# A two-part graph network kernel: PSUM columns in node order, one contiguous one-hot per edge tile

## The reference

```python
def _layer(h, src, dst, norm, n_nodes, W, b, g, be):
    h = h @ W
    msg = h[src] * norm[:, None]
    h = jax.ops.segment_sum(msg, dst, num_segments=n_nodes) + b
    h = jnp.tanh(h)                      # then LayerNorm, * g + be
...
h = jnp.maximum(_layernorm(x), 0.0)
x = x + gcn(h)                           # two _layer, with self loops
h = jnp.maximum(_layernorm(x), 0.0)
msg = jax.nn.relu(h[src] + edge_attr)
aggr = jax.ops.segment_sum(msg, dst)
out = x + (h + relu(relu((h + aggr) @ W1 + b1) @ W2 + b2))
```

## Time and profile before

| | |
|---|---|
| median of 3 runs | 2902.43 us (2901.16 to 2912.98) |
| profiled execution | 2900.96 us, span 2899.1 us |
| busy | PE 2130.6, DVE 2363.1, ACT 2021.1, POOL 1765.8 us |
| granted clock of PE, mean over the span | 0.892 |
| edge multiplications (L1237) | 7500, in two groups of 3750: 1044.3 and 1013.4 us busy |
| one-hots (L918) | 1875, 860.8 us busy |
| DMA | 446.67 MB in 234,030 packets |

### The profile page before, as it was taken

The page is one execution under the profiler, slowest core; times in us unless marked ns, Lnnn a source line. Parts: engine busy times, 40 slices in busy tenths (PEclk is TensorE's granted clock), DMA queues, the critical chain, the costliest instruction groups (busy, mean ns, idle before and its releaser), DMA issues.

```text
span 2899.1 us, 53761 instructions
## 1 busy us (share of the span) xinstructions
PE 2130.6 (73%) x15433; PEld 1913.3 (66%) x15433; DVE 2363.1 (82%) x8137; ACT 2021.1 (70%) x5708; POOL 1765.8 (61%) x2717
## 2 busy tenths in 40 slices
PE   0200039999999957677767778787179999999988
PEld 0100039998889957676667677786168888887877
DVE  4999847887777747999999999999968787777665
ACT  0039967998899666555666666546488999988756
POOL 4025667777777537887667756762077776765540
PEclk9999999999999779777888877768689999999869
DMA  0059945665556443444445444433256665655443
GB/s 14 1 218 381 371 156 144 178 176 169 162 173 178 114 163 108 128 129 142 149 146 146 138 136 152 142 109 124 106 149 176 183 178 173 168 167 156 141 115 102
DMA packets 234030, 446.67 MB, mean 154 GB/s; under 512 B 98093, under 2 KB 99128, under 8 KB 233732
## 3 DMA queue, kind: packets, MB, share of 16 engines
q1 hardware_dynamic: 189193, 374.34, 38.6%
q0 software_dynamic: 43680, 68.58, 11.2%
q10 hardware_dynamic: 859, 0.23, 0.0%
HBM read 286.58 MB, written 156.41 MB: 153 GB/s over the span
## 4 chain that ended last, share of the span: by engine, by line
PE 43%; DVE 35%; ACT 11%; POOL 5%; issue 3%; DMA 2%; SPq 1%; DVEq 0%; ACTq 0%
PE ps L1237 21%; DVE hot_ L918 9%; ACT rows_f_ L1053 6%; PE ps L1272 6%; PE ps L1282 6%; PE ps L1222 5%; PE ps L1253 5%; POOL got_f_ L682 5%; DVE stat_b_ L853 4%; DVE stat_a_ L853 4%; DVE rows_f_ L980 4%; DVE y_f_ L972 2%; DVE hot_p_ L747 2%; DVE low_f_ L892 2%; DVE square_f L833 1%
## 5 line engine op out<-in xcount | busy, mean ns | idle before, releaser
L682 POOL DMA_INDIRECT got_f_<-table,src_of x1365 | 1424.7, 1044 | 751.0 <-issue 370.5
L1237 PE MATMUL ps<-hot_,high_f_ 128*96 128x304 f32 (+46 forms) x3750 | 1044.3, 313 | 285.9 <-DVE hot_ L918 283.9
L1237 PE MATMUL ps<-hot_,low_f_ 128*96 128x304 f32 (+46 forms) x3750 | 1013.4, 308 | 0.0
L1237 PEld LDWEIGHTS ps<-hot_,high_f_ 128*96 128x96 f32 (+1 forms) x3750 | 704.1, 188 | 360.0 <-issue 195.4
L918 DVE TENSOR_SCALAR hot_<-node_at,dst_of 128x368 fp32r<-128x368 f32 (+33 forms) x1875 | 860.8, 498 | 46.7 <-PE ps L1237 42.3
L1237 PEld LDWEIGHTS ps<-hot_,low_f_ 128*96 128x96 f32 (+1 forms) x3750 | 706.5, 188 | 32.0
L1066 ACT COPY z_f_<-ps 97x1024 f32<-97x1024 f32 (+2 forms) x294 | 301.1, 1024 | 365.5 <-PE ps L1237 364.6
L1078 ACT ACTIVATE y_f_<-ps,ds 128x96 f32<-128x96 f32 x1568 | 388.6, 377 | 104.5 <-PE ps L1253 104.4
L1222 PE MATMUL ps<-ident_f,in_f_ 128*97 128x128 f32 (+1 forms) x1568 | 226.3, 292 | 265.3 <-DMA in_f_<-table 265.3
L853 DVE BATCH_NORM_STATS2 stat_a_<-y_f_ 128x6 f32<-128x96 f32 x1952 | 385.7, 245 | 5.9 <-ACT y_f_ L1078 5.8
L1222 PEld LDWEIGHTS ps<-ident_f,in_f_ 128*97 128x97 f32 (+1 forms) x1568 | 198.5, 181 | 265.6 <-DMA in_f_<-table 265.6
(11 more groups left out here) (117 smaller groups left out, 2807.7 us busy)
## 6 DMA issues: line engine op xcount, KB each, us to landing
x_f_<-in_x SPq DMA_DIRECT2D x146, 384.0 KB, 3.9
table<-rows_f_ SPq DMA_DIRECT2D x98, 396.0 KB
in_f_<-table SPq DMA_DIRECT2D x98, 396.0 KB
table<-rows_f_ SPq DMA_DIRECT2D x98, 392.0 KB
in_f_<-table SPq DMA_DIRECT2D x98, 392.0 KB
table<-rows_f_ SPq DMA_DIRECT2D x98, 388.0 KB
in_f_<-table SPq DMA_DIRECT2D x98, 388.0 KB
out<-y_f_ SPq DMA_DIRECT2D x97, 384.0 KB, 4.5
```

The source lines that it names most:

```text
L682: pool.indirect_dma_start(out=got_f[g][:, u * w:(u + 1) * w], out_offset=None, in_=table[:, :], in_offset=bass.IndirectOffsetOnAxis(ap=src ...
L1237: last = pe.matmul(acc[0:w, h, :].rearrange("m (s p) -> m s p", p=P)[:, :, p0:p0 + pw], part[:, u * wide_w:u * wide_w + w], hot_view(slot, ...
```

## The change

PSUM's columns are put in the order of the nodes. For that a partition now holds 4 nodes of the first half of the block (4p to 4p + 3) and 4 of the second (512 + 4p on): the loads and stores move two runs of 4 rows for each partition (`move`), and the degrees' positions are computed with other shifts. A slab is then every fourth column of a bank: the own transposes write PSUM with a stride of 4 words (16 bytes), and the projection and output layer read their weights with that stride. A tile has one contiguous one-hot over its band (cut at block borders only where the band is wider than 1024 nodes), which serves all blocks that the tile touches; its buffer is free again after the last of them. PE multiplies one contiguous piece for each bank that the tile touches, twice for high and low. Bands are rounded to 2 nodes.

```diff
-                lo = max(first, int(lo) // (2 * slabs) * 2 * slabs)
-                hi = min(stop, -(-math.ceil(hi) // (2 * slabs)) * 2 * slabs)
+                lo = max(first, int(lo) // 2 * 2)
+                hi = min(stop, -(-math.ceil(hi) // 2) * 2)
...
-                    for b in range(lo // block, -(-hi // block)):
-                        p0, p1 = (max(lo, b * block) - b * block) // slabs, (min(hi, (b + 1) * block) - b * block) // slabs
-                        use.append((place[b], q, u, b, p0, p1 - p0))
+                    cuts = [lo, hi] if hi - lo <= block else [lo, *range((lo // block + 1) * block, hi, block), hi]
+                    for lo, hi in zip(cuts, cuts[1:]):
+                        k = len(self.tiles)
+                        self.tiles.append((q, u, lo, hi))
+                        use += self.uses(place, block, k, lo, hi)
...
+    def uses(self, place, block, k, lo, hi):
+        found = []
+        for b in range(lo // block, -(-hi // block)):
+            pieces = []
+            for h in range(2):
+                bank = b * block + h * block // 2
+                c0, c1 = max(lo, bank), min(hi, bank + block // 2)
+                if c0 < c1:
+                    pieces.append((h, c0 - bank, c1 - c0, c0 - lo))
+            found.append((place[b], k, pieces))
+        return found
...
+        def move(eng, i, table, tile, done, load, whole=True):
+            lo = plan.at[i] * BLOCK
+            if whole or lo + BLOCK <= N:
+                far = table[ds(lo, BLOCK), :].rearrange("(h p q) d -> p h (q d)", h=2, q=S // 2)
+                near = tile[:, :, :].rearrange("p (h q) d -> p h (q d)", h=2)
+                eng.dma_start(near if load else far, far if load else near).then_inc(done, 16)
+                return
+            ...
+        def slab_cols(t, h):
+            return t[:, h * HB:(h + 1) * HB].rearrange("m (p q) -> m q p", q=S // 2)
...
-                for m in plan.pairs_at[i]:
-                    q, u, b, p0, pw = plan.pairs[m]
-                    slot, turn = hot_slot(layer, m)
+                for k in plan.tiles_at[i]:
+                    q, u, lo, hi = plan.tiles[k]
+                    slot, turn = hot_slot(layer, k)
...
                     if turn >= HOTS:
-                        dve.wait_ge(pair_done, turn - HOTS + 1)
+                        b_layer, b_k = divmod(turn - HOTS, TILES)
+                        dve.wait_ge(pair_done, b_layer * PAIRS + plan.last_of[b_k] + 1)
                     c = plan.quads[q][1] + u
-                    dve.tensor_scalar(hot_view(slot, pw), node_at[:, :, 0:pw], float(b * BLOCK + p0 * S),
-                                      dst_of[:, c:c + 1], ALU.add, ALU.is_equal).then_inc(hot_ready_f, 1)
+                    dve.tensor_scalar(hot[slot][:, 0:hi - lo], node_at[:, 0:hi - lo], float(lo), dst_of[:, c:c + 1],
+                                      ALU.add, ALU.is_equal).then_inc(hot_ready_f, 1)
...
-                    k = s % 4 * P
-                    last = pe.matmul(acc[0:w, s // 4, k:k + P], own[:, s, 0:w], ident_f[:, :], start=s % 4 == 0,
+                    to = acc[0:w, s // 4, :].rearrange("m (p q) -> m q p", q=S // 2)[:, s % 4, :]
+                    last = pe.matmul(to, own[:, s, 0:w], ident_f[:, :], start=s % 4 == 0,
...
-                    for h in range(2):
+                    for h, c0, n, a in pieces:
                         for part in (high_f[f], low_f[f]):
-                            last = pe.matmul(acc[0:w, h, :].rearrange("m (s p) -> m s p", p=P)[:, :, p0:p0 + pw],
-                                             part[:, u * wide_w:u * wide_w + w],
-                                             hot_view(slot, pw)[:, h * S // 2:(h + 1) * S // 2, :],
+                            last = pe.matmul(acc[0:w, h, c0:c0 + n], part[:, u * wide_w:u * wide_w + w],
+                                             hot[slot][:, a:a + n], start=False,
...
-                    last = pe.matmul(to[:, s // 4, s % 4 * D:(s % 4 + 1) * D], z_f[i % 2][0:w, s * P:(s + 1) * P],
+                    last = pe.matmul(to[:, s // 4, s % 4 * D:(s % 4 + 1) * D], slab_cols(z_f[i % 2][0:w, :], s // 4)[:, s % 4, :],
...
-                    last = pe.matmul(ps[3][:, s // 4, s % 4 * D:(s % 4 + 1) * D], hid_f[i % 2][:, s * P:(s + 1) * P],
+                    last = pe.matmul(ps[3][:, s // 4, s % 4 * D:(s % 4 + 1) * D], slab_cols(hid_f[i % 2], s // 4)[:, s % 4, :],
```

More of the change, by code:

```diff
@@ L130, in __init__ @@
         self.first_place = [place[b] for b, _ in supers]
-        self.quads, self.pairs, self.pairs_at, use = [], [], [[] for _ in range(blocks)], []
+        self.quads, self.tiles, self.pairs, self.pairs_at, use = [], [], [], [[] for _ in range(blocks)], []
         for i in self.order:
@@ L209, in gnn_kernel @@
     TILES_MAX = CHUNK
+    TILES = len(plan.tiles)
+    assert all(plan.last_of[k - HOTS] < plan.first_of[k] for k in range(HOTS, TILES))
+    assert max(hi - lo for _, _, lo, hi in plan.tiles) <= BLOCK
     assert GROUPS4 == 4 and SUPERS <= 128 and all(plan.pairs_at) and plan.at.index(BLOCKS - 1) >= X_RING + Y_RING
@@ L507, in table_written, with moved, hot_slot @@
                 eng.wait_ge(stored[j], stored_before(stage + 1, j))
[L509 to L514, removed]
+        def move(eng, i, table, tile, done, load, whole=True):
[5 more added lines that the diff above has]
+                return
+            for h in range(2):
+                rows_n = min(HB, N - lo - h * HB)
+                parts = rows_n // (S // 2)
+                far = table[ds(lo + h * HB, rows_n), :].rearrange("(p q) d -> p (q d)", q=S // 2)
+                near = tile[0:parts, h * (S // 2):(h + 1) * (S // 2), :].rearrange("p q d -> p (q d)")
+                eng.dma_start(near if load else far, far if load else near).then_inc(done, 16)
+        def moved(i, ring):
+            turns = range(i % ring, i + 1, ring)
+            return 16 * (len(turns) + (plan.at.index(BLOCKS - 1) in turns))
+        def hot_slot(layer, k):
+            n = layer * TILES + k
             return n % HOTS, n
+        def slab_cols(t, h):
+            return t[:, h * HB:(h + 1) * HB].rearrange("m (p q) -> m q p", q=S // 2)
         def quad_slot(layer, q):
@@ L625, in fast_sync @@
                     sp.wait_ge(out_done, k + 1)
-                    parts = parts_at(k)
-                    sp.dma_start(rows(out, plan.at[k], parts),
-                                 y_f[k % Y_RING][0:parts, :, :].rearrange("p s d -> p (s d)")
-                                 ).then_inc(out_stored[k % Y_RING], 16)
+                    move(sp, k, out, y_f[k % Y_RING], out_stored[k % Y_RING], False, whole=False)
             for j in range(Y_RING):
-                sp.wait_ge(out_stored[j], 16 * len(range(j, BLOCKS, Y_RING)))
+                sp.wait_ge(out_stored[j], moved(BLOCKS - 1 - (BLOCKS - 1 - j) % Y_RING, Y_RING))
         def prologue_pool(pool):
@@ L1229, in gather_edges @@
                 for m in plan.pairs_at[i]:
-                    q, u, _, p0, pw = plan.pairs[m]
-                    slot, turn = hot_slot(layer, m)
+                    k, pieces = plan.pairs[m]
+                    q, u, _, _ = plan.tiles[k]
+                    slot, turn = hot_slot(layer, k)
                     f, quad_turn = high_slot(layer, q)
```

50 lines of the change are left out of this document (24 added, 26 removed).

## The result

The changed kernel takes 3457.6 us (median of 4 runs, 3448.9 to 3461.0) against 2901.9 for the kernel before on the same chip: ratio 1.191, 95% interval 1.188 to 1.193. The forecast was 2852 with a range from 2822 to 3005. The rival nearest to the time, strided weights at half rate, had a chance of 0.18 and said 3207 (about 3350 if strided transposes cost as much too); the time lies above both. The counts came out as worked out (5382 edge multiplications, 1644 one-hots). The profiled execution has a span of 3454.9.

The account below looks back on a forecast made before the run. No engine bounds the whole: ACT and DMA fill stage 0, POOL paces layer 0, DVE layer 1, PE layer 2. Terms -10 - 17 - 26 + 3 = -50 gave 2901 - 50 + 1.5: 2852 us, range 2822 to 3005.

Parts of the forecast that it names:

- strided weights at half rate: Rival: projection and output-layer weight loads double; +136, +30, +136 us in layers 0, 1, 2, giving 3207 us; chance 0.18.
- Strides, PE: PE's strided transpose writes to PSUM and strided weight loads in projection and output layer: no cost, 0 taken.
- The end that I gave, doubling: Upper end for PE's strides: 85 us a layer for transposes, 168 us a layer for weights.
- A new wait: DVE waits for one-hot buffers held until a tile's last block; layer 1, bounds 0 and 15 us, 3 taken.
- the 3 us: Cost taken in layer 1 for one-hot buffers held into a second block.
- what the sum said: All terms together, over stage 0 and three layers: -50 us.
- I take 10, bounds 3 and 20: Layer 0, paced by POOL: 10 us saved in the tail and a quicker follow-up to late gathers.
- Layer 1: 17: 17 us saved: 10 from fewer DVE one-hots, 7 from the block of 43 tiles; bounds 5 to 25.
- Layer 2: 26: 26 us saved from fewer PE edge multiplications, with ACT close behind; bounds 15 to 38.
- Stage 0: +3: Loading node rows in smaller DMA pieces costs 3 us, bounds 0 and 15.

Follow-up runs that it names:

- experiment 1: The changed kernel with contiguous weight loads again, the 16-byte stride moved to ACT's copy out of PSUM: 3026.4 us, ratio 1.043.
- experiment 4: The kernel before with projection and output-layer weights read at every second word (8 bytes): 2913.7 us; at every eighth word (32 bytes): 3432.0 us.
- experiment 3: The kernel before with only the own transposes writing PSUM at every fourth word: 2899.6 us, ratio 0.999.
- the two numbered kernels: Tiles numbered in building order, in the change with strided weights (3262.9 us) and in the change with contiguous weights and ACT's strided copy (2846.3 us).
- Experiment 2: The kernel before with only projection and output-layer weights read at every fourth word (16 bytes): 3382.0 us, ratio 1.165.
- renumbered change: The changed kernel, strided weights kept, with its tiles numbered in the order DVE builds them: 3262.9 us, ratio 1.124.
- experiments 6 and 7: Tiles numbered in building order: contiguous weights 2846.3 us, the change 3262.9, cut at blocks 2854.4; old numbers, contiguous weights, only PE's wait count mended: 2857.5 us.

## Why the prediction was wrong

Three parts make the result, each from two kernels: strided weights 3262.9 - 2846.3 = +417; numbering 3457.6 - 3262.9 = +195; and the rest of the change 2846.3 - 2900.2 = -54. Together +558, against 3457.6 - 2901.9 = +556. The parts hardly depend on their order: with the old numbering the strides cost 431 (experiment 1), and without them the numbering costs 180.

**The step that failed: "*Strides, PE* ... I take 0", for the weights.** I argued from rates: PE's loads run at 0.9 ns a column, half of what its port does with other work, so one more slot would fit. The load had no such room at a step of 16 bytes: it took 121 ns more, 233 instead of 112. The end that I gave, doubling, was the right size, and PE's projections in layer 0 cost 182 us more against my 168. The rows that I weighed least, DVE's with 219 against 182 ns for a step of 396 bytes and none for 8 bytes, had the same shape as the answer: nothing at 8 bytes, a price from somewhere above. The Trainium skill, "SBUF — State Buffer", Door 1: The DMA port swizzle, with its 16-byte lines, fits the table of experiment 4 for weight loads; I had put its consequence at 0.18. For the strided PSUM writes I took 0 and that held, but the argument was the same one from rates that failed for the weights, so it held by luck. For these transposes the rule of the Trainium skill, "PSUM — Partial Sum Buffer", Specifications (TRN2), that any non-contiguous access slows matmuls, is not borne out (experiment 3, 109 ns with and without).

**The rival's price was mis-sized too.** It said +136, +30 and +136 net of the PE work saved, so 168 gross in layers 0 and 2; between the two numbered kernels it is +159, +8 and +259. Layer 1 hides nearly all of it in PE's waits. In layer 0 PE has 182 us more of projections and 15 us more of transposes and edge multiplications, and 38 us of that go into its old idle time. In layer 2 the output layer's 179 us bring another 85: PE's edge multiplications go from 297 to 342 us and its transposes from 81 to 121, in number the same. They are slower because the granted clock falls (0.96 to 0.86 in the windows): these two kinds run about 220 us at the lower level against 32. For the transposes this accounts for the whole: 83 us more of them run at the lower level, at 213 instead of 109 ns a start, which is 41 us. Experiment 2, where the stride is the only edit, has the same drop (0.86 in layer 2 against 0.94 in the earlier trace rows), and of its 53 falls in that layer 52 begin in the strided loads or in the transposes behind them. So the fall comes with the strided loads; what about them brings it was not tried. The clock also fell further in experiment 2's layer 0 (0.87) than in the renumbered change's (0.91), which is part of why the strides cost 480 us there and 417 here.

**The step that was missing: "*A new wait* ... bounds 0 and 15".** I looked at the wait that the change shows, DVE's for a buffer, and asked how long it holds. The other end of the same ring, PE's count of ready one-hots, changes its meaning without a changed line: the count was the place in the building order and became the number of the tile. No rival held it. It cost 180 to 195 us (experiments 6 and 7). As for the buffer that I did price: the kernel that holds one-hots over two blocks is 8 us faster than the one that doesn't (2846.3 and 2854.4; their intervals overlap), so there is nothing to be seen of the 3 us.

**What held.** Without those two, and with the stride moved to ACT, the change does what the sum said, -54 against -50 (2846.3; forecast 2852). That the total fits within 4 us is in part luck, since two terms miss in opposite ways:

- Layer 0: "I take 10, bounds 3 and 20", measured 651.8 to 651.2, -1. POOL paces it: last gather at 999.5 and 995.5 before. PE's edge time fell by 19 us there (328 to 309, where I had 32) and its waits took them up (PE waits 53 us for one-hots where it waited 31). Under the lower bound.
- Layer 1: 17, measured 20 (1047.2 to 1027.5). DVE busy 983 to 974. Right size, though 77 one-hots fewer are only a part of it.
- Layer 2: 26, bounds 15 and 38, measured 36 (798.9 to 763.0). PE's edge time fell by 31 us and ACT's rate was no bar: ACT is busy 284 in 300 against 277 and waits 73 us for sums against 101.
- Stage 0: +3, measured +0.8.

So the counts were right, and so was which engine paces which layer; two terms are off by some 10 us each in opposite ways. The loss came from one unit price, read off an analogy where no row had it, and from one wait.

## What to carry to other kernels

When a kernel's order of building changes, check both ends of every counted semaphore: a wait for `number + 1` is right only while numbers follow the order in which things are made, and a count that is merely too high gives the right output and only costs time, here 1.7 to 1.8 us each time. Where no row shows a strided operand on the engine in question, a price per column with a doubling at the end deserves a larger chance than a rate that seems to leave room suggests. The nearest strided row on another engine is a warning and no price: it pointed the right way for the weights and the wrong way for the PSUM writes, and one small kernel with the stride alone (experiments 2 and 3) tells. And if a stride has to be somewhere, put it where the measurement says it is free, here ACT's read of PSUM or PE's write to it.

## What the runs showed of the hardware

- PE's fp32 weight loads of 128 columns take 112, 118, 233 and 239 ns for words 4, 8, 16 and 32 bytes apart at the upper level of the clock. At the lower level the first two take 213 and the others what they took at the upper: two different limits, of which only one goes with the clock.
- Beside such strided loads the granted clock falls though PE is busy: in layer 2 of the renumbered change 65 falls, all in the strided loads or right behind them, against 5 with contiguous weights.
- PE's fp32 transposes that write PSUM 16 bytes apart, and ACT's copy that reads PSUM 16 bytes apart, show no price (109 ns; 1018 against 1024 ns).
- Nearly twice as many packets for the same bytes (41,487 against 22,105 in 160 us, their times 105.6% against 100.3% of the 16 engines' span) still moved 60 MB in that time. A load of x took 9.7 instead of 5.2 us from issue to landing, and the stage's end moved by 0.8 us.
